# Attention 1 of a two-layer gated cross-attention and mixture-of-experts kernel: a reordered beginning, heads normalised once per unit, and the columns of x centred and scaled on VectorE

## The reference

```python
def _layernorm(x, axis=-1, eps=1e-05):
    m = jnp.mean(x, axis=axis, keepdims=True)
    v = jnp.var(x, axis=axis, keepdims=True)
    return (x - m) / jnp.sqrt(v + eps)
...
def _L1_xattn_ref(q, k, v, Wc, bc):
    b, s, _ = q.shape
    qh = q.reshape(b, s, N_GROUPS, HEADS_PER_GROUP, HEAD_DIM).transpose(0, 2, 3, 1, 4)
    kh = k.reshape(b, s, N_GROUPS, HEAD_DIM).transpose(0, 2, 1, 3)
    vh = v.reshape(b, s, N_GROUPS, HEAD_DIM).transpose(0, 2, 1, 3)
    scores = jnp.einsum('bghsd,bgtd->bghst', qh, kh) * scale
    probs = jax.nn.softmax(scores, axis=-1)
    out = jnp.einsum('bghst,bgtd->bghsd', probs, vh)
    out = out.transpose(0, 3, 1, 2, 4).reshape(b, s, D_MODEL)
    return out @ Wc.T + bc
```

## Time and profile before

| | us |
|---|---|
| median of 3 runs | 2227.23 |
| lowest and highest run | 2224.43, 2231.81 |
| the profiled execution, its own time | 2224.05 |
| its span, first to last instruction | 2222.2 |
| mean granted clock of TensorE, as a share of 2.4 GHz | 0.923 |
| busy: PE, DVE, ACT, POOL | 1907.8, 1152.9, 891.1, 967.7 |

### The profile page before, as it was taken

The page is one execution under the profiler, slowest core; times in us unless marked ns, Lnnn a source line. Parts: engine busy times, 40 slices in busy tenths (PEclk is TensorE's granted clock), DMA queues, the critical chain, the costliest instruction groups (busy, mean ns, idle before and its releaser), DMA issues. The chain is left out here.

```text
span 2222.2 us, 36653 instructions
## 1 busy us (share of the span) xinstructions
PE 1907.8 (86%) x10825; PEld 1568.1 (71%) x10825; DVE 1152.9 (52%) x2331; ACT 891.1 (40%) x1466; POOL 967.7 (44%) x703
## 2 busy tenths in 40 slices
PE   4578999979892778898778999999999889999995
PEld 2256778767671456665556777899998789899994
DVE  4835564423333998888855666444443334344442
ACT  5652122123342787877733122233332223233331
POOL 5353755625452677878710100233332423333441
PEclk8779999989995789998889999999999999999997
DMA  9376766889978674325531000946489895754444
GB/s 343 121 251 213 216 206 217 284 293 241 283 172 163 177 227 107 47 40 117 183 121 48 21 30 19 370 83 166 79 243 316 235 307 99 209 111 78 79 82 110
DMA packets 131464, 372.74 MB, mean 168 GB/s; under 512 B 20456, under 2 KB 24424, under 8 KB 126104
## 3 DMA queue, kind: packets, MB, share of 16 engines
q1 hardware_dynamic: 82616, 261.73, 36.8%
q0 software_dynamic: 33600, 79.73, 19.0%
q10 hardware_dynamic: 15072, 29.04, 3.6%
HBM read 209.93 MB, written 151.86 MB: 163 GB/s over the span
## 5 line engine op out<-in xcount | busy, mean ns | idle before, releaser
L1681 PE MATMUL ps<-f_wb,f_xThi 128*128 x2088 | 539.6, 340 | 28.6 <-issue 23.1
L1805 POOL DMA_INDIRECT y_scratch<-f_yo,f_rows x150 | 239.4, 1596 | 491.8 <-issue 281.0
L1681 PEld LDWEIGHTS ps<-f_wb,f_xThi 128*128 128x128 f32 x2088 | 373.7, 194 | 40.7 <-issue 31.7
L1681 PE MATMUL ps<-f_wb,f_xTlo 128*128 x1044 | 347.9, 333 | 0.0
L752 POOL TENSOR_TENSOR a_elo<-a_e,a_ehi 128x1024 f16<-128x1024 f32 x128 | 282.2, 2217 | 82.7 <-ACT a_ehi L821 80.4
L1700 PE MATMUL ps<-f_wb,f_hThi 128*128 (+2 forms) x822 | 279.4, 421 | 6.5 <-DVE f_hTlo L2080 6.5
L2098 DVE TENSOR_TENSOR f_g<-ps,f_bb 128x352 f32<-128x352 f32 x111 | 58.3, 525 | 342.6 <-PE ps L1681 342.6
L1778 POOL DMA_INDIRECT f_xg<-xn_scratch,f_rows x150 | 159.9, 1066 | 157.4 <-PE ps L1665 114.8
L1516 ACT ACTIVATE f_yo<-ps,f_share 128x512 f32<-128x512 f32 x150 | 103.3, 689 | 253.9 <-PE ps L1700 189.8
L1681 PEld LDWEIGHTS ps<-f_wb,f_xTlo 128*128 128x128 f32 x1044 | 201.6, 193 | 0.0
L1002 DVE TENSOR_REDUCE a_nmax<-ps 128x1 f32<-128x512 f32 x256 | 164.0, 681 | 36.2 <-PE ps L855 35.9
(11 more groups left out here) (241 smaller groups left out, 3607.0 us busy)
## 6 DMA issues: line engine op xcount, KB each, us to landing
f_wb<-w_scratch SPq DMA_DIRECT2D x16, 2816.0 KB
w_scratch<-f_stage_up SPq DMA_DIRECT2D x27, 1024.0 KB, 5.4
w_scratch<-a_stage_up SPq DMA_DIRECT2D x23, 1024.0 KB, 5.3
f_stage_raw<-in_f_w_dram SPq DMA_DIRECT2D x29, 768.0 KB, 7.4
f_wb<-w_scratch SPq DMA_DIRECT2D x16, 1024.0 KB
w_scratch<-f_stage_down SPq DMA_DIRECT2D x108, 128.0 KB, 2.3
f_wb<-w_scratch SPq DMA_DIRECT2D x8, 1536.0 KB, 10.2
a_later_raw<-in_f_w_dram SPq DMA_DIRECT2D x16, 768.0 KB, 5.1
```

What stands on the lines that cost most here:

```text
L1681: mm = pe.matmul(out, xt[:, b % 2, k, :], weights(at, w, k, low), start=(m == 0), stop=(m == 3 * KD - 1))
L1805: pool.indirect_dma_start(y_d, bass.IndirectOffsetOnAxis(ap=rows_of[:, b:b + 1], axis=0), yo[:, b % 3, :], None, bounds_check=ROWS + SPARE ...
```

## The change

1. `row_stats` of batch 1 leaves the block of mixture 0 and stands in VectorE's list of attention 1, behind `prepare_vector` of unit 1. Those of batches 2 and 3 are no longer made by BN_STATS: ScalarE sums each row of x (`means`, L791 of the changed kernel) and its squared deviation (`spreads`, L800) with the accumulating output of ACTIVATE, 16 instructions of 128x512, takes one square root for both, and VectorE makes `rstd` and `nbias` of them (`row_factors`, two small instructions a batch). A one-element exponential (`warm`) stands before unit 0.
2. The columns of units 0, 1 and 4 to 15 are made by VectorE (`columns_vector`, four TENSOR_SCALAR of 128x128, L1078 of the changed kernel), those of unit u + 4 at the end of step j = 5. The columns of units 2 and 3 stay with ScalarE.
3. SP copies the strips of unit 0 before it loads the keys of unit 1.
4. The sum of the exponentials is carried in each of the three parts of V (99 columns instead of 97), `osum` holds all four heads of a unit, and one reciprocal and one multiplication over 128x512 (`heads_vector`) per unit take the place of four and four. It stands in step j = 2 of the unit behind.
5. `JOBS` moves every turn and tile one place (half a unit) later; the last two turns of the last batch go to banks of their own.

```diff
@@ JOBS
-        JOBS = {(2, 6): ("turn", 0, 0), (3, 2): ("turn", 0, 1), (3, 6): ("turn", 0, 2), (0, 2): ("turn", 1, 3),
-                (0, 6): ("tile", 1, 0), (1, 2): ("tile", 1, 1), (1, 6): ("tile", 1, 2), (2, 2): ("tile", 1, 3)}
+        JOBS = {(3, 2): ("turn", 0, 0), (3, 6): ("turn", 0, 1), (0, 2): ("turn", 1, 2), (0, 6): ("turn", 1, 3),
+                (1, 2): ("tile", 1, 0), (1, 6): ("tile", 1, 1), (2, 2): ("tile", 1, 2), (2, 6): ("tile", 1, 3)}
@@ SP
                 load(0, 0)
+                strips(0, 0)
                 load(1, 1)
-                strips(0, 0)
                 strips(1, 1)
@@ ScalarE
+            def means(act, b):
+
+                act.wait_ge(g["x_back"][b], 16)
+                wait(act, spread_ready, TB * (b - 2))
+                for t in range(TB):
+                    n = TB * (b - 2) + t
+                    wait(act, mean_ready, n)
+                    act.activation(t_out[:], x[:, TB * b + t, :], ACT.Identity, scale=-1.0 / D,
+                                   accum_out=nmean[:, b, t:t + 1]).then_inc(mean_ready, 1)
+
+            def spreads(act, b):
+
+                for t in range(TB):
+                    n = TB * (b - 2) + t
+                    act.wait_ge(mean_ready, TB * (b - 1))
+                    wait(act, spread_ready, n)
+                    act.activation(t_out[:], x[:, TB * b + t, :], ACT.Square, bias=nmean[:, b, t:t + 1],
+                                   accum_out=squares[:, b, t:t + 1]).then_inc(spread_ready, 1)
...
                 act.wait_ge(g["s_ln"], 2 * B + 1)
-                for u in range(2):
-                    columns_scalar(act, u, u, 0)
+                prepare_scalar(act, 0, 0)
                 keys_scalar(act, 0, 0)
+                prepare_scalar(act, 1, 1)
+                columns_scalar(act, 2, 2, 0)
                 keys_scalar(act, 1, 1)
-                prepare_scalar(act, 0, 0)
-                columns_scalar(act, 2, 2, 0)
-                prepare_scalar(act, 1, 1)
                 columns_scalar(act, 3, 3, 0)
+                g["deviation"](act, 2, 1)
                 prepare_scalar(act, 2, 2)
-                g["deviation"](act, 2, 2)
+                means(act, 2)
                 act.wait_ge(v_in, 16 * B)
                 act.copy(v_hi, v_raw).then_inc(vhi_ready, 1)
+                spreads(act, 2)
+                means(act, 3)
                 act.wait_ge(vres_ready, 1)
                 act.copy(v_mid, v_res).then_inc(vmid_ready, 1)
+                spreads(act, 3)
+                act.wait_ge(spread_ready, 2 * TB)
+                act.activation(deviations[:, 2:4, :], squares[:, 2:4, :], ACT.Sqrt, scale=1.0 / D,
+                               bias=eps[:, 0:1]).then_inc(dev_ready, 2)
+                act.activation(warm[:], eps[:, 0:1], ACT.Exp, scale=0.0)
                 maxima_scalar(act, 0, 0)
...
-                        if j == 4 and not (isinstance(u, int) and u + 4 >= UNITS):
-                            columns_scalar(act, u + 4, grp, b + 1)
@@ VectorE
-                dve.reciprocal(rden[:], out[:, :, 3 * HD]).then_inc(rden_ready, 1)
-                dve.tensor_reduce(osum[:], out[:, :, 0:3 * HD].rearrange("p t (c d) -> p t d c", c=3), AX.X,
+                dve.tensor_reduce(osum[:, :, q, :], out[:, :, 0:VC].rearrange("p t (c d) -> p t d c", c=3), AX.X,
                                   ALU.add).then_inc(sum_ready, 1)
...
+            def heads_vector(dve, u, grp):
+
+                dve.wait_ge(sum_ready, HPG * u + HPG)
+                dve.reciprocal(rden[:], osum[:, :, :, HD]).then_inc(rden_ready, 1)
+                dve.wait_ge(rden_ready, u + 1)
+                dve.tensor_tensor(otok[:, :, P * grp:P * grp + P].rearrange("p t (q d) -> p t q d", q=HPG),
+                                  osum[:, :, :, 0:HD], rden[:].unsqueeze(3).to_broadcast([P, TB, HPG, HD]),
                                   ALU.mult).then_inc(o_ready, 1)
...
+            def columns_vector(dve, u, grp, b):
+
+                wait(dve, q_tr, u - 1)
+                for t in range(TB):
+                    T = TB * b + t
+                    dve.tensor_scalar(xc[:, grp % 2, t, :].rearrange("p (d q) -> p d q", q=HPG),
+                                      x[:, bass.ds(T, 1), P * grp:P * grp + P]
+                                      .rearrange("p o (q d) -> p (o d) q", q=HPG),
+                                      rstd[:, bass.ds(T, 1)], nbias[:, bass.ds(T, 1)], ALU.mult,
+                                      ALU.add).then_inc(xc_ready, 1)
...
+                columns_vector(dve, 0, 0, 0)
+                columns_vector(dve, 1, 1, 0)
                 prepare_vector(dve, 0, 0)
                 prepare_vector(dve, 1, 1)
+                dve.wait_ge(g["x_back"][1], 16)
+                g["row_stats"](dve, 2, 1)
                 prepare_vector(dve, 2, 2)
-                dve.wait_ge(g["x_back"][2], 16)
-                g["row_stats"](dve, 2, 2)
                 maxima_vector(dve, 0, 0, range(16))
                 parts_vector(dve, 0, 0)
-                dve.wait_ge(g["x_back"][3], 16)
-                g["row_stats"](dve, 2, 3)
+                for b in range(2, B):
+                    row_factors(dve, b)
                 maxima_vector(dve, 1, 1, range(8))
...
-                        if head:
-                            head_vector(dve, *head)
+                        if head and head[2] == HPG - 1:
+                            heads_vector(dve, *head[:2])
                         stage.low(dve, *split_step(u, j, LOWER))
+                        if j == 5 and isinstance(u, int) and u == GROUPS - 1:
+                            dve.wait_ge(factor, 4)
+                        if j == 5 and not (isinstance(u, int) and u + 4 >= UNITS):
+                            columns_vector(dve, u + 4, grp, b + 1)
```

More of the change, by code:

```diff
@@ L123, in deviation @@
         def deviation(act, nth, b):
-            act.wait_ge(s_var, B * nth + b + 1)
+            act.wait_ge(s_var, nth_of(nth, b) + 1)
             act.activation(std[:], vraw[:], ACT.Sqrt, scale=1.0 / D, bias=eps[:, 0:1]).then_inc(s_std, 1)
         def normalise(act, xn, t, T, nth, s_xn):
-            act.wait_ge(s_ln, B * nth + 1)
+            act.wait_ge(s_ln, nth_of(nth, 0) + 1)
             act.activation(xn[:, t, :], x[:, T, :], ACT.Identity, scale=rstd[:, bass.ds(T, 1)],
@@ L520, in cross_attention_1 @@
 def cross_attention_1(nc, a, sb, g):
-    x, ident, gates, rstd, nbias, ps = (g[k] for k in ("x", "ident", "gates", "rstd", "nbias", "ps"))
+    x, ident, gates, rstd, nbias, eps, ps = (g[k] for k in ("x", "ident", "gates", "rstd", "nbias", "eps", "ps"))
     UNITS = B * GROUPS
-    VC = 3 * HD + 1
+    VH = HD + 1
+    VC = 3 * VH
     A_BANK, PV_BANK, MISC = 4, 6, 7
@@ L554, in cross_attention_1 @@
         elo = sb(ctx, "a1_elo", [P, 4, 2, S], F16)
-        osum = sb(ctx, "a1_osum", [P, TB, HD])
-        rden = sb(ctx, "a1_rden", [P, TB])
+        osum = sb(ctx, "a1_osum", [P, TB, HPG, VH])
+        rden = sb(ctx, "a1_rden", [P, TB, HPG])
         otok = sb(ctx, "a1_otok", [P, TB, D])
@@ L561, in cross_attention_1 @@
         t_out = sb(ctx, "a1_tout", [P, D])
+        nmean = sb(ctx, "a1_nmean", [P, B, TB])
+        warm = sb(ctx, "a1_warm", [P, 1])
+        squares = sb(ctx, "a1_squares", [P, B, TB])
+        deviations = sb(ctx, "a1_deviations", [P, B, TB])
         stage = g["Stage"](ctx, "a1_stage_", raw=later_raw)
@@ L568, in cross_attention_1 @@
         v_in = sem("v_in")
+        mean_ready, spread_ready, dev_ready, factor = (sem(n) for n in ("mean", "spread", "dev", "factor"))
         k_in, strips_in, m_in = ([sem(f"{n}{i}") for i in range(2)] for n in ("k_in", "strips_in", "m_in"))
@@ L729, in cross_attention_1 @@
             v_raw, v_res = (m[:].rearrange("p t (g d) -> p t g d", g=GROUPS) for m in (vraw, vres))
-            v_hi, v_mid, v_lo = (v3[:, :, :, HD * i:HD * i + HD] for i in range(3))
+            v_hi, v_mid, v_lo = (v3[:, :, :, VH * i:VH * i + HD] for i in range(3))
             @block.gpsimd
@@ L783, in maxima_scalar, with turn_scalar @@
                 act.copy(mhi[:, grp % 2, :], ps[0:HPG * TB, MISC, 0:P]).then_inc(mhi_ready, 1)
-            def turn_scalar(act, b, k):
+            def turn_scalar(act, b, k, bank=MISC):
                 act.wait_ge(o_tr, GROUPS * b + k + 1)
-                act.copy(oT[:, :, k, :], ps[:, MISC, :].rearrange("p (t s) -> p t s", t=TB)).then_inc(oT_ready, 1)
+                act.copy(oT[:, :, k, :], ps[:, bank, :].rearrange("p (t s) -> p t s", t=TB)).then_inc(oT_ready, 1)
             @block.scalar
@@ L835, in _ @@
                 batches(act, unit)
-                turn_scalar(act, B - 1, GROUPS - 1)
+                turn_scalar(act, B - 1, GROUPS - 2, A_BANK)
+                turn_scalar(act, B - 1, GROUPS - 1, A_BANK + 1)
                 for b in range(B - 1):
@@ L1384, in rows_scalar @@
                 def rows_scalar(b):
-                    act.wait_ge(g["s_ln"], B * NTH + b + 1)
+                    act.wait_ge(g["s_ln"], g["nth_of"](NTH, b) + 1)
```

(8 more changed lines are left out.)

42 lines of the change are left out of this document (23 added, 19 removed).

## The result

The changed kernel takes **2279.51 us** (median of four runs, 2277.06 to 2286.62) against 2227.61 for the kernel before beside it: ratio **1.0252**, 95% interval 1.0211 to 1.0294. The medians are 52 us apart; their quotient, 1.0233, isn't the recorded ratio but lies inside its interval. Timed again in a later series, the ratio was 1.0202 (1.0166 to 1.0238). The forecast was 2270 with a range of 2206 to 2290.

A forecast was written before the change was run, and what follows sets the result against it. No single engine bounds attention 1; with four nearly equally busy, the waits decide. Beginning +2, columns +48, last batch -7, last head step +0.5 make +43.5 on 2224.05: 2267.6, so a median of 2270, range 2206 to 2290.

The forecast's parts named there:

- The likeliest case: Columns on VectorE wait for POOL's subtractions and the kernel gets slower: 2245 to 2292 us, chance 0.60.
- The chain: Waits lead back to mixture 1's first weight load; what attention 1 gains or loses goes one for one into the total.
- The beginning, +2: Start of attention 1 up to the first exponential, with mixture 0 ending 4.1 us earlier: +2 us, bounds -8 and +7.
- The columns, +48 for units 0 to 11: VectorE's four column instructions in step 5 wait for POOL: +4.0 us for each of 12 units, bounds -1.6 and +6.
- The factor 0.82: POOL is idle 18% of batch 1, and groups meeting it idle cost nothing extra: 4.8 us a unit becomes 4.0.
- The last batch, -7: Units 12 to 15, without columns: VectorE's 2.7 us saved on heads credited for 2.6 of 4 units, bounds -1 and -11.
- Turns and tiles, nothing: Later turns and tiles only move work by half a unit: no effect on the time.
- The sum: +2 + 48 - 7 + 0.5 = +43.5 us on the profiled 2224.05: 2267.6, forecast for the median 2270.
- R1: Rival: strided column reads use one port and never meet POOL, so faster: -20.5 us, 2207 us; chance 0.25.
- R2: Rival: one wait for POOL per column group, 2.2 us a group, +0.4 a unit: no change, 2228 us; chance 0.15.
- R3: Rival: ScalarE's statistics passes hide under the maxima, beginning -8: 2260 us, counted inside the 0.60 of the likeliest case.
- The signs: Profile: L1078 well over 1 us, first exponential about 732.6, units 4 to 11 24 to 28 us, ScalarE idle 6 or more.

The follow-up runs named there:

- the two executions compared above: Changed kernel with columns back on ScalarE, once with heads normalised one by one (0.9992 of the kernel before), once with heads per unit (0.9955).
- the 31 x 4 kernel: Changed kernel whose columns of units 4 to 15 leave out the last of each head's 32 elements: 0.9987 of the kernel before.

## Why the prediction was right

The likeliest case came true: slower, by the wait of VectorE's columns for POOL. Point by point:

- **The chain.** One for one, as said: of 57.2 us at the start of mixture 1, none was won back later.
- **The beginning, +2.** Measured +1.7, with `qhi`, V, `mhi` and the first exponential each within 0.8 us. That `mhi` came out to the tenth is luck: V landed 0.8 later than forecast, and ScalarE's list from there to `mhi` took 15.8 us where I had 16.6. A pass with its read takes 0.91 us for the squares, as I had from rows 5, but 0.76 for the sums, which I had at the same price. That the square root of batch 1 stood behind a load of keys was overlooked; it had no price, since ScalarE's list was later still.
- **The columns, +48 for units 0 to 11.** Measured 8.9 + 24.6 + 21.7 = 55.2. (4.8 x 0.82 is 3.9, so the 48 was 47 before rounding.) The total is nearer than its parts: by the forecast each batch loses 16 us, batch 0 lost 7 less and the other two 14 more together. The mechanism is the one forecast, down to "four instructions that each let one pass": in unit 6 I had a group of 5.4 us from 18.2 us into the unit, and it is 5.2 from 18.3. Three sizes were off. The factor 0.82 for groups that meet POOL idle has no ground in batches 1 and 2, where every group had a queue; from start to end they take 6.3 us on average in batch 1. Batch 0 is the other way, its groups take 3.1. And the 3.4 us from the end of `mlo` to the next exponential, which before was the shortest of these gaps (mean 4.2), became up to 6.9 in units 5 and 6, in part because TensorE had stood for the sum behind the group (with the sum ahead of the group 5.2 and 5.4 are left, and why they are more than before stays open): a waiter that I had named nowhere, though my own list said that the sum of head 1 stands between the columns and `mlo`.
- **The last batch, -7.** This step failed: measured -0.5, and the heads per unit alone make this batch 1.5 us longer (94.4 against 92.9). I credited all of the 2.7 us of VectorE, with the argument that its list is full there. It is full of instructions that wait for POOL in their turn; part of each wait taken away is, by the two executions compared above, paid by another of them, and the rest did not shorten the batch. Why not stays open. In batches 1 and 2 the credit was right in kind: 1.3 us a unit.
- **Turns and tiles, nothing.** Together with the beginning 0.9992, so nothing that the medians can tell. By the stages of one execution each, batches 0 to 3 changed by -4.0, +0.5, -2.6 and -2.1 us, 8 us in all; batch 0 of the change itself differed by 1.7 between two executions. Whether "nothing" was right stays open.
- **The sum.** +43.5 against 57.2 by the traces (1.7 + 55.2 - 0.5, and 0.7 at the end where I had 0.5) and 52 by the medians, or 49 in the later series. The columns were 7 us too low and the last batch 6.5. That 2279.5 lies within 2206 to 2290 says little, since that range holds the main part of all three cases; that it lies within 2245 to 2292 says more.
- **R1** fell by the form that I named for it: as the waits for POOL and the shortest times show, this pattern, with 32 and 128 as outermost sizes, takes both ports, and the one with 31 does not. What R1 would have given is seen in the 31 x 4 kernel: 0.9987, where I had 2207 us, 0.991. By the traces that kernel loses 3.5 us in attention 1 where R1 gains 20.5. A group of 1.7 us instead of 1.1 makes 7 of these 24 us and the last batch 5.5; where the rest lies stays open. **R2** fell in batches 1 and 2, where a group takes 5.2 to 7.6 us; the groups of 3.1 us in batch 0 look like it. **R3** was a part that could have been had, but not by this list: the passes did not hide.
- **The signs.** L1078 has a mean of 1.30 us, POOL waits 132.8 us for ScalarE's tiles and not 80.4, and the first exponential of unit 0 comes at 732.6, as said. Units 4 to 11 were put at 24 to 28 us and take 26.7 to 30.9. ScalarE is idle for more than 6 us before the first exponential of four units only (6, 7, 10 and 11).

## What to carry to other kernels

Where two engines exclude each other, as VectorE's columns and POOL's subtractions do here, an instruction costs up to one of the other engine's each time it is issued, so four small ones of 0.4 us took 5.2 to 7.6 us beside a queue of 2.1 us subtractions; count instructions, not elements, and before moving work to a less busy engine, look at who stands behind it in that engine's list on the way to the next unit. A wait of this kind that is taken from one instruction may be paid in part by the next, as in batch 3; credit it only where nothing else of that kind follows. A source of 31 rows of 4 with a destination in one run of 124 kept these instructions clear of POOL for 0.1 us each, but it leaves out one element in 32; a form that makes all of them and stays clear was not tried.
